# The first block's chains on VectorE as single operations woven between its two parts, identity products in TensorE's waits, and new order tables

## The reference

```python
x = L0_attn_x                                   # (1, 2048, 256), float32
x = x + _layernorm(attn(_layernorm(x)))         # attention block, with its own MLP inside
x = x + _layernorm(ffn(_layernorm(x)))          # mixture of 8 experts, top 2, and a shared expert

# attn(x), 16 heads of 16
h = layernorm(x, ln1); x_conv = silu(causal_conv4(h) + conv_b)
q, k = l2norm(h @ Wq), l2norm(h @ Wk); v = layernorm(h @ Wv)          # per head
u = sigmoid(x_conv @ Wig + big) * k * v
mem = scan over time of mem[t] = gamma[t] * mem[t-1] + u[t]           # gamma = sigmoid(x_conv @ Wg + bg)
out = layernorm_per_head(layernorm_per_head(mem) * q) * gnw + gnb
h = x + (out * sigmoid(x_conv @ Wog + bog)) @ Wo
return h + (silu(h2 @ Wgate) * (h2 @ Wval)) @ Wout                     # h2 = layernorm(h)

# ffn(x): shared expert 256->704->256, gated by a sigmoid; router softmax, top 2 of 8, experts 256->176->256
```

## Time and profile before

| | |
|---|---|
| Three runs | 584.18, 586.59, 586.7 us |
| Profiled execution | 583.73 us, its span 582.0 us |
| TensorE busy, and its weight loads | 509.6 us (88%), 399.8 us (69%) |
| VectorE busy | 403.5 us (69%) |
| ScalarE busy | 262.7 us (45%) |
| GpSimd busy | 107.2 us (18%) |
| Chain that ended last | TensorE 69%, VectorE 20%, ScalarE 5% |

### The profile page before, as it was taken

How to read it: one execution, slowest core, us unless ns; L and a number is a source line. 1 busy time by engine, 2 the same in 40 slices (tenths; PEclk the granted TensorE clock), 3 DMA queues, 4 the chain that set the end, 5 groups by cost and what they waited for, 6 DMA issues and landing times.

```text
span 582.0 us, 8039 instructions
## 1 busy us (share of the span) xinstructions
PE 509.6 (88%) x2384; PEld 399.8 (69%) x2384; DVE 403.5 (69%) x1237; ACT 262.7 (45%) x475; POOL 107.2 (18%) x133
## 2 busy tenths in 40 slices
PE   2970697999399999999999997999998899999970
PEld 1530454777276778876687786888876799999850
DVE  6899874799955979954858962515557567676467
ACT  4722565344565332764504147111334456666404
POOL 1420004000014140004050000050013034444400
PEclk9995789999699999999999998999988999999996
DMA  8951000010200020110010101020139234444184
GB/s 289 404 188 31 8 0 0 1 36 2 72 1 1 9 102 0 63 48 0 1 65 10 36 2 36 2 73 1 36 96 290 60 93 121 131 127 129 67 288 144
DMA packets 29628, 44.52 MB, mean 77 GB/s; under 512 B 3163, under 2 KB 24283, under 8 KB 29243
## 3 DMA queue, kind: packets, MB, share of 16 engines
q1 hardware_dynamic: 24595, 33.07, 18.0%
q0 software_dynamic: 3408, 9.38, 4.4%
q10 hardware_dynamic: 1584, 1.57, 0.9%
HBM read 27.67 MB, written 16.34 MB: 76 GB/s over the span
## 4 chain that ended last, share of the span: by engine, by line
PE 69%; DVE 20%; ACT 5%; issue 3%; DMA 2%; POOL 0%; SPq 0%; ACTq 0%; POOLq 0%; DVEq 0%
PE psum L840 15%; PE psum L799 12%; PE psum L801 11%; PE psum L800 11%; PE psum L871 7%; PE psum L895 3%; PE psum L809 3%; PE psum L891 2%; PE psum L1026 1%; PE psum L1009 1%; DMA YF<-y_routed 1%; PE psum L914 1%; DVE est L1159 1%; DVE SM L1484 1%; ACT QKV L639 1%
## 5 line engine op out<-in xcount | busy, mean ns | idle before, releaser
L704 ACT ACTIVATE SM<-psum 128x512 f32<-128x512 f32 (+1 forms) x56 | 33.0, 594 | 125.2 <-PE psum L801 106.9
L1484 DVE TENSOR_TENSOR SM<-SM,psum 128x512 f32<-128x512 f32 (+1 forms) x56 | 38.2, 683 | 47.9 <-ACT SM L704 47.8
L577 POOL DMA_INDIRECT x_dispatched<-XN,dest x32 | 32.0, 1002 | 156.8 <-DVE XN L1552 148.3
L840 PE MATMUL psum<-WOU,SM 128*128 128x256 f32 x256 | 60.1, 379 | 0.3 <-DVE SM L1484 0.3
L840 PEld LDWEIGHTS psum<-WOU,SM 128*128 128x128 f32 x256 | 48.0, 189 | 9.8 <-issue 2.6
L568 POOL TENSOR_TENSOR QKV<-QKV,hvec 128x256 f32<-128x256 f32 x16 | 11.6, 728 | 215.2 <-ACT IG L646 182.8
L871 PE MATMUL psum<-WQKV,HT 128*128 128x512 f32 (+1 forms) x128 | 47.4, 520 | 3.6 <-ACT QKV L639 1.8
L586 POOL DMA_INDIRECT y_routed<-GO,g_dest x39 | 37.8, 968 | 68.3 <-ACT GO L774 68.0
L840 PE MATMUL psum<-SDN,SM 128*128 128x256 f32 (+1 forms) x192 | 45.0, 383 | 0.0
L871 PEld LDWEIGHTS psum<-WQKV,HT 128*128 128x128 f32 x128 | 25.4, 204 | 24.2 <-issue 19.4
L840 PEld LDWEIGHTS psum<-SDN,SM 128*128 128x128 f32 (+1 forms) x192 | 36.2, 191 | 6.6 <-issue 1.0
(11 more groups left out here) (309 smaller groups left out, 1301.7 us busy)
## 6 DMA issues: line engine op xcount, KB each, us to landing
XG<-x_dispatched SPq DMA_DIRECT2D x39, 130.0 KB, 2.6
YF<-y_routed SPq DMA_DIRECT2D x8, 512.0 KB, 7.1
RUPR<-rup SPq DMA_DIRECT2D x1, 2816.0 KB
X<-x SPq DMA_DIRECT2D x4, 512.0 KB, 6.9
x_after_attention<-X SPq DMA_DIRECT2D x4, 512.0 KB, 2.9
QKV<-x ACTq DMA_DIRECT2D x3, 512.0 KB, 3.3
y_shared<-SH SPq DMA_DIRECT2D x3, 512.0 KB, 2.9
SHF<-y_shared SPq DMA_DIRECT2D x1, 1536.0 KB, 19.4
```

The costliest lines, as they stand in the source:

```text
L577: nc.gpsimd.indirect_dma_start(XD[:, :], bass.IndirectOffsetOnAxis(dest[:, i, old + j:old + j + 1], 0), XN[:, j, :], None).then_inc(dispat ...
L704: nc.scalar.activation(SM[0:rows, g % 3, 0:tb], p_pair(n)[0][0:rows, 0:tb], ACT.Silu).then_inc(silu_ready, 1)
L840: last = nc.tensor.matmul(p_down[:, j // 2, (j % 2) * D:(j % 2 + 1) * D], SM[0:rows, g % 3, j * P:(j + 1) * P], weight[0:rows, m, :], star ...
L1484: nc.vector.tensor_tensor(SM[0:rows, g % 3, 0:tb], SM[0:rows, g % 3, 0:tb], value_rows(n, rows)[:, 0:tb], ALU.mult).then_inc(hid_ready, 1)
```

## The change

Five things change together.

1. `FIRST` for VectorE names single operations: `rs` 1 becomes `rs` 1 to 8, `rstd` becomes `nr` 0 to 7 (first norm) and `gr` 0 to 7 (second), `mean` is two steps, `ln2` becomes `st2`, `lr` and `sh2`. They are interleaved between the parts a and b. The convolution goes on chunk by chunk.
2. Waits for everything (`settle()`) in these steps become waits for the one result that is needed (`after`).
3. `BUSY` puts products identity x identity, whose result nobody reads, ahead of nine steps of TensorE: 26, 9, 10, 46, 16 and 8 in block 0, and 6, 4 and 2 around the stop between block 0 and block 1.
4. `FIRST` for all engines goes on into block 1 (its projections and the first two up-products), in another order; on ScalarE the silu of block 0 stands ahead of the copies of the projections, and the split of `wvl` ahead of `mt`.
5. `PLACE` has new numbers for blocks 1 to 3 on all engines.

```diff
 PLACE = {
     "pe": [
-        [0, 2, 2, 2, 2, 2, 2, 3, 3, 3, 3, 4, 4, 4, 6, 6, 10, 10, 11, 11, 12, 16, 16, 16, 16, 16, 16, 16, 16, 16, 18, 18,
...
+        [2, 2, 2, 2, 2, 2, 2, 2, 2, 2, 2, 2, 3, 3, 3, 5, 5, 5, 5, 9, 9, 12, 12, 12, 12, 12, 14, 16, 16, 16, 21, 21, 21,
...
 FIRST = {
     "pe": """
-        ht:0 q:0 q:1 q:2 q:3 g:0 g:1 g:2 ut:0a ut:0b mt:0a mt:0b og:0a og:0b wo:0a wo:0b ht:+0 h2:0a h2:0b""",
+        ht:0 q:0 q:1 q:2 q:3 g:0 g:1 g:2 ut:0a ut:0b mt:0a mt:0b og:0a og:0b wo:0a wo:0b ht:+0 h2:0a h2:0b q:+0 q:+1
+        q:+2 mup:0 q:+3 mup:1""",
...
+BUSY = {
+    ("ht", 0, 0, 0): 26, ("ut", 0, 0, 0): 9, ("mt", 0, 0, 1): 10, ("og", 0, 0, 0): 46, ("og", 0, 0, 1): 16, ("h2", 0, 0, 0): 8,
+    ("ht", 2, 0, 0): 4, ("xt", 0, 0, 0): 6, ("h2", 1, 0, 0): 2,
+}
+BUSY_BANK = {"ht": 7, "q": 7, "ut": 6, "mt": 0, "og": 2, "wo": 4, "h2": 6}
...
+                if b == 0 and (stage, b, m, part) in BUSY:
+                    if stage == "ut":
+                        pe.wait_ge(qkv_copied, new)
+                    if stage in ("mt", "og", "wo"):
+                        pe.wait_ge(gate_ready, {"mt": C, "og": 2 * C, "wo": 3 * C}[stage])
+                    if stage == "h2":
+                        pe.wait_ge(mem_ready, C)
+                for _ in range(BUSY.get((stage, b, m, part), 0)):
+                    bank = BUSY_BANK[stage] + part if b == 0 and stage != "xt" else 2
+                    nc.tensor.matmul(psum[:, bank, 0:P], ident[:, :], ident[:, :], start=True, stop=True)
                 if (stage, m) == ("ht", 0):
...
+                if stage in ("nr", "gr"):
+                    ins = root(m, ("root", part), *scratch(G, part), mu[:, per_group])
+                    if m == 7:
+                        step(ins)
+                        mark("mu", part)
...
                 if stage == "norm":
-                    settle()
+                    after("mu", part)
...
+                if (stage, m) == ("st2", 0):
+                    dve.wait_ge(hr_ready, u + 1)
+                    for j in mine:
+                        step(nc.vector.bn_stats(st[:, j, :], HR[:, j, :]))
+                    mark("root", part)
...
+                if stage == "lr":
+                    ins = root(m, ("root", part), *scratch(len(mine), part), l2r[:, t0:t1])
```

More of the change, by code:

```diff
@@ L160 @@
-        h2:1b conv:+1 conv:+2 conv:+3""",
+        ln0:0 ln0:1 ln0:2 conv:0 conv:1 conv:2 conv:3 split:0 q:0 q:1 rs:0a rs:1a q:2 rs:2a rs:3a rs:4a q:3 rs:5a
+        rs:6a rs:0b rs:1b rs:7a rs:8a rs:2b rs:3b u:0a u:1a rs:4b u:2a u:3a rs:5b rs:6b rs:7b rs:8b u:0b u:1b u:2b
+        u:3b scan:0a scan:1a scan:0b scan:1b var:0a nr:0a nr:1a nr:2a nr:3a nr:4a nr:5a nr:6a nr:7a norm:0a affine:0a
+        affine:1a var:0b nr:0b nr:1b mean:1a nr:2b nr:3b mean:2a nr:4b nr:5b nr:6b nr:7b centre:1a norm:0b affine:0b
@@ L161 @@
+        affine:1b mean:1b mean:2b centre:1b var:1a gr:0a gr:1a var:1b gr:2a gr:3a gr:4a gr:0b gr:5a gr:6a gr:1b gr:7a
+        gr:2b norm:1a gr:3b gr:4b gr:5b gr:6b gr:7b norm:1b ln0:+0 o:0a ln0:+1 o:0b ln0:+2 wo:0a st2:0a st2:1a st2:2a
+        lr:0a lr:1a lr:2a wo:0b lr:3a st2:0b st2:1b st2:2b lr:0b lr:4a lr:5a lr:1b lr:2b lr:6a lr:7a sh2:0a lr:3b
+        lr:4b lr:5b lr:6b lr:7b sh2:0b conv:+0 conv:+1 conv:+2 h2:1a conv:+3 h2:1b split:1 q:+0 q:+1 q:+2 q:+3 mup:0
+        mup:1""",
     "pool": """
[L162 removed]
+        q:0 q:1 q:2 q:3 q:+0 q:+1 q:+2 q:+3""",
@@ L173, in steps @@
 def steps(engine):
-    yield from first(engine)
+    begun = list(first(engine))
+    yield from begun
     attention = [(PLACE[engine][b - 1][i], s[0], b + (s in AHEAD), s[1], 0) for b in range(1, NB)
                  for i, s in enumerate(ATTENTION) if b + (s in AHEAD) < NB]
+    attention = [s for s in attention if s[1:] not in begun]
     for n, step in enumerate(ORDER):
```

82 lines of the change are left out of this document (57 added, 25 removed), and 46 rows, old and new, of the table PLACE.

## The result

The changed kernel takes 579.49 us in the median of four runs (579.07 to 580.82), the kernel before 586.64 beside it (584.18 to 586.94): a ratio of 0.9891, with a 95% interval of 0.986 to 0.9922. Over both, twelve runs of the changed kernel lie between 578.43 and 584.18 with a median of 579.6, so the change is worth about 0.9%, some 5 us. The profiled execution took 579.6 us (span 577.9) against 583.73 (582.0) before: a lead of 4.1 us, less than the medians show, because the profiled run of before was one of its quickest.

The account below looks back on a forecast made before the run. TensorE was taken as the bound, VectorE in the first block. Terms 2.8 + 2.0 - 0.8 + 1.8 - 1.0 + 0.8 = 5.6 us took 583.73 to 578.1, put at 579.0 for the median; 8-in-10 range 573.5 to 585.

Parts of the forecast that it names:

- The start: Up to the first scan: warm projections and woven VectorE steps bring it from 38.33 to 35.5, gain 2.8 us.
- The rival of a cold start: Early products bring no warmth, the scan stays near 38.6; gain falls to 2.5 us, 581.2 us; chance 0.13.
- The first block's chains: First scan through second norm in block 0: interleaving at about 9 places saves 1.0 us.
- that rival: VectorE gains nothing by weaving, its pipeline emptying after each operation anyway; 581.0 us; chance 0.09.
- Second layer norm: Block 0: interleaving saves 0.75 us, the earlier ScalarE split and shorter transposes 0.25.
- The cold transposes: Block 0 output gates: 16 products between both parts' transposes, if cold, delay part b; -0.8 us, bounds 0 and -1.6.
- Block 1's projections: New order up to block 1's gates saves waits, a slow q start and PSUM hand-overs; gain 1.8 us.
- The new wait at u of block 1: TensorE reaches u's transposes before VectorE has u: 1.3 us new wait against 0.3 that goes, -1.0.
- The stop: Output projections of block 1 to router logits: clock returns sooner, router and first q lose less; +0.8 us, bounds 0 and 2.
- The tables of blocks 2 and 3: New placing there brings no TensorE wait and no gain: 0 us, bounds +1 and -4.
- The slower rival: New tables make VectorE's chain 3 us late in each of blocks 1 to 3; 588.6 us; chance 0.05.
- the rival of a larger gain: u arrives in time (1.0), output gates stay warm (0.8), tables take another 1 us: 575.5 us; chance 0.16.

Follow-up runs that it names:

- every wait for the newest: The changed kernel, same order, but each wait for one named VectorE result waits for all VectorE instructions so far; 586.11 us, 1.0021 to the kernel before.
- the second trace: The changed kernel itself, unaltered, measured and profiled again on another chip; 580.44 us, 0.9929 to the kernel before.
- the longer fill: The changed kernel with 64 instead of 46 products ahead of part a's output-gate transposes in block 0, 2 instead of 16 ahead of part b's; 581.61 us, 0.9948.

## Why the prediction was right, and where it was not

The time (579.0 against 579.49 and 580.44) and the direction came out. Step by step, in the time of the profiled pair:

*The start, 2.8: measured 2.16* (38.33 to 36.17). The theory of warmth held: from first product to gates the projections take 10.39 us (13.44 before, 13.06 in the kernel without products), the loads 0.19 from 13.26 on. TensorE began q at 12.76 and its gates at 23.15 where I had 12.4 and 22.7, and VectorE ended u at 36.06, not 35.2; the two meet. The missed cost is GpSimd, whose products of v and q lie beside VectorE's reciprocal roots from 24.3 to 28.5: five operations take 0.58 to 0.77 instead of 0.23. The trace of before had this to be read: the product on 128x512 that scales `QKV` took 1.13 us at 27.41 beside GpSimd, and 0.68 at 35.55 without it. Of the 2.27 us at the scan itself the order alone gives 0.71, the products alone 0.44 (table), in a trace whose projections were partly cold. The rival of a cold start is refuted for the changed kernel: transfers are the same (378 GB/s for 384) and the pace is full, and taking the products out brings the slow pace back. So where granted clock (1.00) and pace (half) disagreed before 19 us, the pace was the truth. The products don't ensure it: in two other kernels that have the 26 (products only, every wait for the newest) the projections took 12.25 us. An identity product took 0.227 us (46 in 10.44), where I had 0.21.

*The first block's chains, 1.0: measured 1.1* (the lead of 3.27 at VectorE's last norm, 61.27 to 58.00, less 2.16). From the scan to the norm's end the kernel without products has it too (21.84 us for 22.85), the products alone do not (24.46), and the one with every wait for the newest loses it (23.30). So the weaving, and in it the waits, is shown as the cause, and that rival is refuted. *Second layer norm, 1.0 in all: measured 0.8* (VectorE's first sum with the output product went from 67.20 to 64.75, a lead of 2.45; q has 3.29).

*The cold transposes, -0.8: measured -0.8* (3.27 to 2.45), but 2.2 in the second trace (66.14), past its bound of 1.6. I had put this down to the clock. The larger part is the place: products between the two parts hold the second whatever their pace. In the first trace of the longer fill, with 2 there instead of 16, VectorE's first sum is at 63.74 and the lead whole (3.46).

*Block 1's projections, 1.8: measured 1.8* (3.29 to 5.10), and 1.8 without products; with the old lists and the products it is -0.2, so the new order is the cause.

*The new wait at u of block 1, -1.0: it did not come.* There is 0.42 at the second gate and nothing at 100.54; the lead falls by 0.2 to the output projections. I had VectorE's u 12.8 us behind the end of q3, with ScalarE's copy and square, and TensorE there after 11.5. Measured from the end of q3 (88.62) it is 11.8 for VectorE (100.41) and 11.9 for TensorE (100.54): the sum of what follows "directly, with copy and square" was 1.0 too long. The tables do cost something in block 1 that I hadn't seen: 0.9 us from the gates to the output projections, by the run with the old ones.

*The stop, +0.8: measured -0.6* (lead 4.87 to 4.31). This is the step that failed. The rows of before showed that VectorE's chain sets the stop, and I said so; I still counted a gain at the router. With 4, 6 and 2 products the clock came up at 152.0, fell again at 155.4 and was at half under the router, as it was without them. Before, it came back behind three of the router's six records, here only with the sixth, and that is where most of the 0.56 went. A gain of 0.8 was not to be had: with a full clock all through, the stop is 0.35 us shorter than before.

*The tables of blocks 2 and 3, 0: measured -0.2* behind the logits, and -0.3 in the run with the old ones. The slower rival is refuted: no wait of TensorE over 1 us stands between 170 and 340.

The sum of the trace is 2.16 + 1.11 - 0.82 + 0.84 + 1.81 - 0.23 - 0.56 - 0.21 = 4.1 us, against 5.6. The two errors of the stop (1.4 too much) and the start (0.6) were partly paid for by the wait that didn't come (0.8). That the median still met the forecast owes something to luck. Of the 1.5 us of gain that did not come, 0.9 is made good by what I added for the median, and this was not needed: the profiled run, 579.6, lies at its median of 579.49. And the gain between medians, 7.1 us on one chip and 4.0 on another, is not the 4.1 of one pair of executions: the profiled run of before was quick, 583.73 where its median was 586.6 on one chip and 584.3 to 585.1 on others. Two slips of the working change nothing: rows 4 give 148.84 for the fall of the clock, not 148.92, and the rival of a larger gain comes to 575.3, not 575.5.

## What to carry to other kernels

Products that keep TensorE warm pay where the engine would begin real work cold and another engine has work meanwhile (2.7 us in the first projections here, of which 1.6 reach the scan); between two halves of one chain they are themselves a delay, at half pace twice as long. Before filling a wait, ask who sets its end: where VectorE's chain does, a full clock in it is worth only what follows. And interleave two dependent chains on VectorE with waits for the one result that is needed: order without those waits gave nothing here (23.30 us against 22.85 unwoven).
